# Scan products on VectorE, early gates on GpSimd and an earlier turned input in a two-layer recurrent kernel

## What is computed

```python
xr = x @ W_in;  x_in, res = halves of xr          # 256 channels each
xc = silu(causal depthwise conv(x_in, 4 taps))
p = xc @ W_x;  delta = softplus(p[:16] @ W_dt + b_dt);  Bm = p[16:32];  Cm = p[32:]
h = h * delta + B * x                             # scan over the tokens; 16 states, summed
s = ((h.sum * C_t) * silu(res)) @ W_out
probs = softmax(x @ router_w.T); gate = the four largest of 16, the rest 0
f = sum over 2 shared experts of gelu(x @ up) @ down
  + sum over 16 routed experts of (gelu(x @ up) * gate) @ down
```

## Time and profile before

| | us |
|---|---|
| median of three runs | 760.62 |
| the profiled execution | 760.88 |
| its span in the profile | 759.1 |
| TensorE matmul busy | 649.5 |
| VectorE busy | 671.9 |
| ScalarE busy | 506.1 |
| GpSimd busy | 339.0 |

### The profile page before, as it was taken

The page is one execution under the profiler, slowest core; times in us unless marked ns, Lnnn a source line. Parts: engine busy times, 40 slices in busy tenths (PEclk is TensorE's granted clock), DMA queues, the critical chain, the costliest instruction groups (busy, mean ns, idle before and its releaser), DMA issues. The chain is left out here.

```text
span 759.1 us, 10868 instructions
## 1 busy us (share of the span) xinstructions
PE 649.5 (86%) x2711; PEld 300.9 (40%) x2711; DVE 671.9 (89%) x1435; ACT 506.1 (67%) x800; POOL 339.0 (45%) x310
## 2 busy tenths in 40 slices
PE   3795999999999975679989989988988988998985
PEld 1342444444444433234434434433433433443432
DVE  4996999999999997498999899898999999999885
ACT  2472566666766653786776777678678678677774
POOL 6446567776777640134224323423423423432341
PEclk9898999999999998799999999999999999999998
DMA  6430000000000000000000000000000000000000
GB/s 156 109 85 14 0 0 0 0 0 0 0 0 0 1 0 1 0 2 0 15 14 1 14 14 0 15 14 0 14 14 14 0 14 14 0 14 14 0 15 28
DMA packets 10740, 11.29 MB, mean 15 GB/s; under 512 B 4800, under 2 KB 6288, under 8 KB 10720
## 3 DMA queue, kind: packets, MB, share of 16 engines
q1 hardware_dynamic: 9744, 10.73, 4.9%
q0 software_dynamic: 112, 0.33, 0.2%
q10 hardware_dynamic: 864, 0.00, 0.1%
HBM read 6.87 MB, written 4.19 MB: 15 GB/s over the span
## 5 line engine op out<-in xcount | busy, mean ns | idle before, releaser
L1057 PE MATMUL bank<-arena,w 128*128 128x512 f16 x640 | 153.9, 389 | 20.2 <-DVE arena L723 14.1
L1057 PE MATMUL bank<-arena,dnT 128*128 128x512 f32 x288 | 145.1, 604 | 23.4 <-DVE arena L944 23.4
L618 ACT ACTIVATE arena<-bank,xinv 128x512 f32<-128x512 f32 x144 | 95.0, 687 | 58.9 <-PE bank L1057 58.8
L1057 PEld LDWEIGHTS bank<-arena,w 128*128 128x128 f16 x640 | 63.4, 100 | 99.2 <-issue 24.6
L441 POOL TENSOR_TENSOR arena<-arena 128x512 f32<-128x512 f32 x48 | 61.1, 1303 | 59.9 <-ACT arena L555 59.9
L451 POOL TENSOR_TENSOR arena<-arena 128x512 f32<-128x512 f32 x32 | 50.1, 1565 | 84.3 <-DVE arena L985 73.8
L431 POOL TENSOR_TENSOR arena<-arena 128x512 f32<-128x512 f32 x16 | 17.5, 1092 | 150.1 <-DVE arena L923 150.1
L1057 PE MATMUL bank<-xh,upH 128*128 128x512 f16 x144 | 55.9, 388 | 29.3 <-ACT arena L618 26.5
L481 ACT ACTIVATE arena<-bank 128x512 f16<-128x512 f32 x96 | 53.9, 606 | 35.0 <-PE bank L1057 35.0
L1057 PEld LDWEIGHTS bank<-arena,dnT 128*128 128x128 f32 x288 | 51.1, 190 | 62.9 <-DVE arena L944 46.4
L944 DVE TENSOR_TENSOR arena<-arena 128x512 f32<-128x512 f32 x80 | 75.8, 965 | 0.0
(11 more groups left out here) (188 smaller groups left out, 1480.2 us busy)
## 6 DMA issues: line engine op xcount, KB each, us to landing
x_all<-in_L_attn_x SPq DMA_DIRECT2D x16, 256.0 KB, 2.7
out<-x_all SPq DMA_DIRECT2D x16, 256.0 KB, 2.0
up_n<-in_L_ffn_routed_up SPq DMA_DIRECT2D x1, 512.0 KB, 3.9
dn_n<-in_L_ffn_routed_down SPq DMA_DIRECT2D x1, 512.0 KB, 5.4
wx<-in_L_attn_W_x SPq DMA_DIRECT2D x1, 288.0 KB, 2.8
k_u<-in_L_ffn_k POOLq DMA_DIRECT2D x1, 256.0 KB, 5.2
w_in<-in_L_attn_W_in SPq DMA_DIRECT2D x1, 256.0 KB, 2.5
k_u<-in_L_ffn_k SPq DMA_DIRECT2D x1, 128.0 KB, 6.0
```

The source lines that it names most:

```text
L618: a.activation(act[:, c, :], q_U[c % 2][:, :], ACT.Gelu, scale=xinv[:, I_UP:I_UP + 1]).then_inc(sem["b_act"], 1)
L1057: return nc.tensor.matmul(ps, lhsT, rhs, start=start, stop=stop)
```

## The change

- The two products `yb` move from GpSimd to VectorE, behind the scans and ahead of the low halves of the conv output.
- GpSimd does gate products 0 to 2, VectorE 3 to 7. VectorE's first two stand behind the normalisation, one behind `output_weight(0)`, and two behind the scan inputs; none is left between the logits and the convolution. The waits of the gelus and of the down products follow.
- `gates_out` moves from the head of the next body to the end of the body, behind the last gelu and ahead of the load of the silu table.
- The next input is turned after up product 4, into bank 3, and its high half is made between gelu 5 and gelu 6. `xh`, `xl` are held twice, and bodies take them in turn.
- TensorE's two step products move ahead of the second residual product. The up products swap their two banks, and the first waits for all six taps.

```diff
--- before.py
+++ after.py
@@ -146,6 +146,8 @@
         xl = sb("xl", [P, N], F16)
+        xh_ = sb("xh_", [P, N], F16)
+        xl_ = sb("xl_", [P, N], F16)
         thf = sb("thf", [P, N])
@@ -434,7 +436,7 @@
                 if has(m):
-                    for c in range(GV, RC):
+                    for c in range(GP):
                         pool.wait_ge(sem["b_act"], UC * m + c + 2)
@@ -443,13 +445,6 @@
                     spread_gates(f)
-                if has(m):
-                    for k in range(IC):
-                        pool.wait_ge(sem["b_cr"], IC * m + k + 1)
-                        pool.wait_ge(sem["b_scan"], IC * m + k + 1)
-                        after(pool, sem["b_s"], m)
-                        g.tensor_tensor(yb[:, k, :], H[:, k, :], cr[:, k, :], ALU.mult).then_inc(sem["b_y"], 1)
-
             bodies(pool, layer1)
@@ -535,11 +530,11 @@
                     last.then_inc(sem["prep_high"], 1)
-            def turned_high(n):
+            def turned_high(n, par=0, ps=q_T):
 
                 actv.wait_ge(sem["b_xnT"], n + 1)
-                after(actv, sem["b_up"], UC * n)
-                a.activation(xh[:, :], q_T[:, :], ACT.Copy, scale=XS).then_inc(sem["b_xh"], 1)
+                after(actv, sem["b_up"], UC * (n - 1))
+                a.activation((xh, xh_)[par][:, :], ps[:, :], ACT.Copy, scale=XS).then_inc(sem["b_xh"], 1)
 
@@ -549,9 +544,9 @@
                 def gates_out():
-                    actv.wait_ge(sem["b_gtT"], m + 1)
-                    after(actv, sem["b_actg"], GV * m)
-                    after(actv, sem["b_actp"], GP * m)
+                    actv.wait_ge(sem["b_gtT"], f + 1)
+                    after(actv, sem["b_actg"], GV * f)
+                    after(actv, sem["b_actp"], GP * f)
                     a.activation(gate[:, :], q_Q[:, :], ACT.Copy).then_inc(sem["b_gate"], 1)
@@ -609,16 +604,14 @@
                     if has(m):
-                        if c > GV:
-                            actv.wait_ge(sem["b_actp"], GP * m + c - GV)
+                        if c > GP:
+                            actv.wait_ge(sem["b_actg"], GV * m + c - GP)
                         elif c:
-                            actv.wait_ge(sem["b_actg"], GV * m + c)
+                            actv.wait_ge(sem["b_actp"], GP * m + c)
                         else:
                             actv.wait_ge(sem["b_down"], UC * m + 1)
-                    a.activation(act[:, c, :], q_U[c % 2][:, :], ACT.Gelu, scale=xinv[:, I_UP:I_UP + 1]).then_inc(sem["b_act"], 1)
-
-                if has(m):
-                    gates_out()
+                    a.activation(act[:, c, :], q_U[(c + 1) % 2][:, :], ACT.Gelu, scale=xinv[:, I_UP:I_UP + 1]).then_inc(sem["b_act"], 1)
+
                 if has(t):
@@ -655,8 +648,9 @@
                         gelu(c)
-                if has(f) and has(f + 1):
-                    turned_high(f + 1)
+                        if c == 5 and has(f + 1):
+                            turned_high(f + 1, 1 - par, q_D[1])
+                    gates_out()
                 a.preload_act_table_set(SILU_SET)
@@ -883,11 +877,11 @@
 
-            def turned_low(n):
+            def turned_low(n, par=0, ps=q_T):
 
                 dve.wait_ge(sem["b_xh"], n + 1)
-                after(dve, sem["b_up"], UC * n)
-                v.scalar_tensor_tensor(xl[:, :], q_T[:, :], XS, xh[:, :], ALU.mult, ALU.subtract).then_inc(sem["b_xl"], 1)
+                after(dve, sem["b_up"], UC * (n - 1))
+                v.scalar_tensor_tensor((xl, xl_)[par][:, :], ps[:, :], XS, (xh, xh_)[par][:, :], ALU.mult, ALU.subtract).then_inc(sem["b_xl"], 1)
 
@@ -985,6 +979,12 @@
 
+                def output(k):
+                    dve.wait_ge(sem["b_cr"], IC * m + k + 1)
+                    dve.wait_ge(sem["b_scan"], IC * m + k + 1)
+                    after(dve, sem["b_s"], m)
+                    v.tensor_tensor(yb[:, k, :], H[:, k, :], cr[:, k, :], ALU.mult).then_inc(sem["b_y"], 1)
+
                 if ahead:
@@ -1009,8 +1009,6 @@
                                     ALU.subtract).then_inc(sem["b_lg"], 1)
-                if has(m):
-                    gated(0)
                 if has(f):
@@ -1020,10 +1018,10 @@
                 if has(m):
-                    gated(1)
-                    gated(2)
+                    gated(GP)
+                    gated(GP + 1)
                     output_weight(0)
-                    gated(3)
+                    gated(GP + 2)
                     cap(0)
@@ -1034,19 +1032,22 @@
                 if has(m):
-                    gated(4)
                     dve.wait_ge(sem["b_b"], m + 1)
...
                     scan_input(1)
+                    gated(GP + 3)
+                    gated(GP + 4)
                     softplus(0)
...
                     state(1)
+                    output(0)
+                    output(1)
                 if has(f):
...
                 if ahead:
-                    turned_low(f + 1)
+                    turned_low(f + 1, 1 - par, q_D[1])
 
@@ -1177,11 +1178,12 @@
                 f, m, t = n, n - 1, n - 2
+                XH, XL = (xh, xh_)[par], (xl, xl_)[par]
 
...
                     w = slice(i * P, (i + 1) * P)
-                    return split3(ps[:, :], w_inH[:, w], w_inL[:, w], xh[:, :], xl[:, :])
+                    return split3(ps[:, :], w_inH[:, w], w_inL[:, w], XH[:, :], XL[:, :])
 
@@ -1214,16 +1216,16 @@
                     else:
-                        pe.wait_ge(sem["b_conv"], IC * f * (TAPS - 1) + CONV_DONE[c])
+                        pe.wait_ge(sem["b_conv"], IC * f * (TAPS - 1) + CONV_DONE[1 - c])
                     w = slice(c * P, (c + 1) * P)
-                    split3(q_U[c % 2][:, :], upH[:, w], upL[:, w], xh[:, :], xl[:, :]).then_inc(sem["b_up"], 1)
+                    split3(q_U[(c + 1) % 2][:, :], upH[:, w], upL[:, w], XH[:, :], XL[:, :]).then_inc(sem["b_up"], 1)
 
...
 
-                    if c > GV:
-                        pe.wait_ge(sem["b_actp"], GP * m + c - GV)
+                    if c > GP:
+                        pe.wait_ge(sem["b_actg"], GV * m + c - GP)
                     elif c:
-                        pe.wait_ge(sem["b_actg"], GV * m + c)
+                        pe.wait_ge(sem["b_actp"], GP * m + c)
                     else:
@@ -1249,12 +1251,16 @@
                         ps = q_Q[:, j * NR:(j + 1) * NR]
-                        mm(ps, xh[:, j::J], rwH[:, :], True, False)
-                        mm(ps, xl[:, j::J], rwH[:, :], False, False)
-                        last = mm(ps, xh[:, j::J], rwL[:, :], False, True)
+                        mm(ps, XH[:, j::J], rwH[:, :], True, False)
+                        mm(ps, XL[:, j::J], rwH[:, :], False, False)
+                        last = mm(ps, XH[:, j::J], rwL[:, :], False, True)
                     last.then_inc(sem["b_rout"], 1)
...
                     residual_in(0)
+                if has(m):
+                    steps(0)
+                    steps(1)
+                if has(f):
                     residual_in(1)
@@ -1267,8 +1273,6 @@
                     expert_out(0)
-                    steps(0)
-                    steps(1)
                     expert_out(1)
@@ -1290,13 +1294,10 @@
                         gates_turned()
-                    if has(f) and has(f + 1) and c == 6:
+                    if has(f) and has(f + 1) and c == 4:
                         pe.wait_ge(sem["b_xn"], f + 2)
-                        if has(m):
-                            pe.wait_ge(sem["b_bx"], IC * m + IC)
-                        else:
-                            pe.wait_ge(sem["b_r"], IC * f + 1)
-                        turn_rows(q_T).then_inc(sem["b_xnT"], 1)
+                        after(pe, sem["b_cr"], IC * (m + 1))
+                        turn_rows(q_D[1]).then_inc(sem["b_xnT"], 1)
                 if has(m):
...
```

## The result

The changed kernel takes 734.35 us (median of four runs, 731.67 to 739.47) against 760.5 us before: a ratio of 0.9655, interval 0.9629 to 0.9681. It is faster by 26 us. The profiled execution's span is 732.7 us, 26.4 less than before.

A forecast was written before the change was run, and what follows sets the result against it. A chain over VectorE, ScalarE and TensorE, router maximum to router maximum, was taken to fill the 27.57 us pass. Removing gated(0)'s slots, 23.8 us together, from 760.88 gave 737.1, or 736.8 us against the median; range 731 to 743.

The forecast's parts named there:

- The chain of four terms: Router maximum to fifth up product 15.46, to w_out 7.56, w_out 1.71, to next maximum 2.84: the whole 27.57 us pass.
- gated(0)'s slot leaves, nothing comes back: VectorE, logits to first tap: 21.77 us saved over bodies 2 to 14, 1.24 in body 1, 0.78 in body 15.
- The reading by the lock alone: Rival: only gated(0)'s wait for GpSimd is saved, its own 0.6 us reappears on the chain; 745 us, chance 10%.
- y products at 0: Two more VectorE products between scans and low halves, 1.2 us, covered because y is ready before w_out; value 0.
- The end of the kernel: Tail: steps waiting for low_z, +0.6 us, offset by y on VectorE; taken as 0, between +0.8 and -0.6.
- the slot of 0.78: Body 15's share of the saving from gated(0) leaving its place on VectorE: 0.86 - 0.08 = 0.78 us.
- Steps ahead of the residual product: TensorE's step products 0.43 us earlier free ScalarE when the taps end; without it the conv silu about 0.6 us late.
- Early input, double halves at 0: Next input turned among the up products, halves held twice: off the chain, 0; bounds +0.6 to -0.5 us a body.
- TensorE "just waits" for gelu(0) instead, value 0: TensorE's 1.67 us stall for gated(1) goes, but gelu(0), bound to the ACT chain, is late next; value 0.
- VectorE's sum: Rival: the busiest engine's total counts, 2.4 us saved a body, giving 728 us; chance 6%.
- the lock at the end of the body: Rival: VectorE's low halves wait for GpSimd's gate products after w_out; +1.7 us a body, 785 us; chance 4%.
- A late gated(6) or (7): Rival: these gate products hold gelu(7), gelu(8) and their expert products, a new wait of the same size; chance 3%.

The follow-up runs named there:

- slot_refilled: The changed kernel with one VectorE gate product (number 3) put back between the logits and the first tap; 758.11 us, ratio 0.9949 to the kernel before.
- gates_only: The kernel before with only the gate products split and placed as in the change, step products left behind expert_out(0); 758.42 us, ratio 0.9965.
- steps_late: The changed kernel with TensorE's step products back behind expert_out(0), as before the change; 755.96 us, ratio 0.9935 to the kernel before.
- y_on_gpsimd: The changed kernel with the two y products moved back to GpSimd; 738.65 us, ratio 0.9706 to the kernel before.
- xch_late: The changed kernel with ScalarE's two conv-output high halves behind gelu(3) and VectorE's caps ahead of gate product 5; 723.46 us, ratio 0.9499 to the kernel before.

## Why the prediction was right

The forecast was 736.8 us in a range of 731 to 743, measured 734.35. By its steps:

- *The chain of four terms*: right. Three kernels that leave out other parts keep the pass at 25.83 to 25.92 in the mean, and the ones that lengthen the chain show it at the full clock, slot_refilled by 0.60 us and gates_only and steps_late by 0.86 and 0.84.
- *gated(0)'s slot leaves, nothing comes back*: right, 21.75 us in bodies 2 to 14 against 21.77. The reading by the lock alone, 745 us, is out: slot_refilled shows the product's own 0.60 us on the chain when it stands there, and off it where the change put it. That it takes 0.69 us there once GpSimd's gate products are done, and 1.78 beside them, agrees with the Trainium skill's rule (SBUF — State Buffer, "Who interferes with whom").
- *y products at 0*: right for the pass, with y ready at 446.01 + 1.26, 2.0 us ahead of w_out, the left end of what was given (19.3 us after the maximum). The end of the kernel was mis-sized: 2.3 us gained from body 15 on instead of 0.8. Of that 1.2 stands in body 15 (maximum to w_out 21.78 before, 20.61 after). It goes with the steps and not with the slot of 0.78 that the prediction counted: gates_only and steps_late, without the slot, take 22.99 and 22.89 there, some 1.2 of it the clock, going by their slowed passes. The other 1.1 is the last w_out and turn at a higher clock, which no term had.
- *Steps ahead of the residual product, "without it the conv silu would be late by about 0.6"*: the mechanism was right, the size was not. It is 0.86 us a pass and, through the clock, some 21 us in all.
- *Early input, double halves at 0*: right within 0.1 us a pass.
- *TensorE "just waits" for gelu(0) instead, value 0*: right, but by luck. TensorE's wait there grew from 1.1 to 1.5 or 1.6 us, and at 2.1 to 2.3 us, half a microsecond more, it costs 1.2 us more in half of the passes or more. The prediction had no term and no rival for the clock. In the profiled execution body 1 paid it and its 1.24 us did not come; in y_on_gpsimd, with the same wait, it did (25.85). That the total is below the forecast nevertheless is body 0 (-1.8) and the end. Of body 0, 1.5 us is the clock coming back sooner in that execution, since y_on_gpsimd took 22.34 for the same program: luck too, and no effect of the change. So the 21.8 us of bodies 2 to 14 are the mechanism, and the 2.5 us by which the total came out below the forecast are small things outside it, more than half of them effects of the clock that had no price.
- *Rivals*: VectorE's sum (728) is out by y_on_gpsimd; the lock at the end of the body did not show, since GpSimd's gates start 0.8 us after w_out, when the low halves have been done for 1.5 us. A late gated(6) or (7) did not show either: from the fifth up product to w_out it is 7.56 us as before.

## What to carry to other kernels

When several engines share one loop, look for the chain that closes on itself in exactly one pass and write down its terms; here a stall off that chain, even 2 us on the busiest engine, was worth nothing, and an operation of 0.6 us on it was worth its length in every pass. Then look at what the edit does to the longest wait of TensorE: shortening a chain elsewhere can lengthen that wait, and a small reordering that keeps it short (two step products here) can be worth as much as the edit it belongs to. Once the chain is written down, the next thing to move can be read from it, as xch_late did.

## What the runs showed of the hardware

TensorE's clock was the surprise. In the same loop, waits of 1.5 to 1.9 us (1.67 before the change, 1.88 in its body 1) left the granted clock at 1.00. Waits of 2.1 to 2.3 us were followed by the 1.2 GHz level in about every second pass of gates_only and steps_late and in nine of thirteen of slot_refilled, for some 3 us; in the passes between, in body 1 of y_on_gpsimd (2.33 us, a pass of 25.85) and of steps_late (2.98 us, 25.84), and in the last full body of the kernel before (2.34 us) the clock held. So the same wait does not always bring it, and what decides between them no run here shows. Filling the wait with products that nobody reads took some 13 us off slot_refilled. The Trainium skill (TensorE: Matmul & The Clock Gate, Part 1) says that "the default state is throttled, and activity releases the throttle"; the runs agree in that, in bodies 2 to 14 of all of them, the level fell only behind TensorE's waits of 2.1 us or more.

The other is the lock between VectorE and GpSimd: operations of VectorE that read two operands in SBUF took 0.6 to 0.7 us clear of GpSimd's products and up to 1.8 beside them. Those that read one operand from PSUM kept their length: in the full bodies before the change sg ran beside GpSimd's gate products, and it took 690 to 695 ns in all 16 bodies that have it.
